# Another order of work for the last three tiles of an attention and sparse-network layer, and the flags' product first in every step

## The reference, cut to what matters

```python
x = x + attention(xn, Wq, Wk, Wv, Wo, rms_w) + ffn(xn, W_syn, b_syn, W_out, b_out, gamma, beta)

# attention: 16 heads of 32, linear attention in chunks of 128 with a decay for each head
inter = einsum('bhcd,bhde->bhce', qi * q_decay, kv)
scores = einsum('bhcd,bhsd->bhcs', qi, ki) * dmask
attn = rms_norm(inter + scores @ vi, rms_w) @ Wo

# ffn: ternary weights, of 2048 values of a row the 204 largest are kept
z = xn @ ternary(W_syn).T + b_syn
thresh = top_k(z, 204)[:, -1:]
hidden = where(z >= thresh, relu(z), 0)
out = layernorm(xn + hidden @ ternary(W_out).T + b_out) * gamma + beta
```

## Time and profile before

| | before |
|---|---|
| median of 3 runs | 943.66 us (943.35 to 943.76) |
| the profiled execution's own time | 945.01 us |
| its span, first to last instruction | 943.2 us |
| busy: TensorE, VectorE, ScalarE, GpSimd | 895.9, 748.7, 728.1, 659.6 us |

### The profile page before, as it was taken

The page is one execution under the profiler, slowest core; times in us unless marked ns, Lnnn a source line. Parts: engine busy times, 40 slices in busy tenths (PEclk is TensorE's granted clock), DMA queues, the critical chain, the costliest instruction groups (busy, mean ns, idle before and its releaser), DMA issues.

```text
span 943.2 us, 22295 instructions
## 1 busy us (share of the span) xinstructions
PE 895.9 (95%) x8307; PEld 437.6 (46%) x8307; DVE 748.7 (79%) x1955; ACT 728.1 (77%) x1321; POOL 659.6 (70%) x588
## 2 busy tenths in 40 slices
PE   4966899999999999999999999999999999999977
PEld 2532544444444444444444444444444444444434
DVE  5898877887777788778777878887787887878875
ACT  6799677987777788777777977777788777778663
POOL 1445578767677777776787777777767777877763
PEclk9989999999999999999999999999999999999999
DMA  9875653445344445534453544435344544444431
GB/s 336 242 190 102 113 102 69 89 91 100 81 84 96 95 63 91 102 83 85 92 101 72 88 91 91 89 81 102 71 87 91 101 80 80 101 87 73 80 77 36
DMA packets 255344, 93.98 MB, mean 100 GB/s; under 512 B 241408, under 2 KB 241664, under 8 KB 254464
## 3 DMA queue, kind: packets, MB, share of 16 engines
q1 hardware_dynamic: 251392, 85.11, 45.5%
q10 hardware_dynamic: 3840, 7.41, 2.2%
HBM read 24.34 MB, written 8.39 MB: 35 GB/s over the span
## 4 chain that ended last, share of the span: by engine, by line
PE 64%; ACT 12%; POOL 11%; issue 8%; DVE 3%; DMA 1%; ACTq 0%; DVEq 0%; POOLq 0%
PE proj L1123 35%; PE p_ffn L1237 8%; PE p_ffn L1267 7%; PE p_wo L1284 6%; ACT Pr L648 3%; PE rows L1193 3%; ACT hl L668 2%; PE rows L1183 2%; POOL area L859 1%; POOL hl L912 1%; DMA area<-in_L_attn_Wk_dram 1%; PE rows L1204 1%; POOL xhl L824 1%; POOL ahl L917 1%; POOL pair_b L936 1%
## 5 line engine op out<-in xcount | busy, mean ns | idle before, releaser
L1123 PE MATMUL proj<-wqkv,xT 128*128 128x512 f16 x1152 | 262.7, 384 | 2.7 <-ACT area L490 2.6
L1123 PE MATMUL proj<-wsynT,xT 128*128 128x512 f16 x1024 | 238.3, 381 | 3.6 <-ACT area L490 3.2
L912 POOL TENSOR_TENSOR hl<-area,hl 128x2048 f16<-128x2048 f32 x31 | 145.2, 4683 | 83.4 <-ACT hl L668 83.4
L1123 PEld LDWEIGHTS proj<-wqkv,xT 128*128 128x128 f16 x1152 | 110.2, 99 | 141.3 <-ACT area L490 14.8
L1123 PEld LDWEIGHTS proj<-wsynT,xT 128*128 128x128 f16 x1024 | 95.1, 98 | 119.6 <-issue 6.0
L1540 DVE SCALAR_TENSOR_TENSOR area<-proj,c,gb 128x512 f32<-128x512 f32 x128 | 95.3, 746 | 25.2 <-PE proj L1123 23.1
L1237 PE MATMUL p_ffn<-woutT,area 128*128 128x512 f16 x480 | 109.7, 379 | 0.0
L1267 PE MATMUL p_ffn<-woutT,area 128*128 128x512 f16 x480 | 108.5, 379 | 0.0
L620 ACT ACTIVATE diag<-ident,c 128x128 bf16<-128x128 f32 x32 | 12.8, 400 | 121.6 <-DVE c L1625 121.6
L1651 DVE MAX8 cand<-area 128x8 f32<-128x128 f32 x512 | 105.3, 277 | 1.1
L1284 PE MATMUL p_wo<-wo,ahl 128*128 128x512 f16 x384 | 88.6, 379 | 3.6 <-POOL ahl L917 2.2
(11 more groups left out here) (264 smaller groups left out, 1766.3 us busy)
## 6 DMA issues: line engine op xcount, KB each, us to landing
xrn<-in_L_attn_x_dram SPq DMA_DIRECT2D x32, 256.0 KB, 3.1
out_dram<-pair_b SPq DMA_DIRECT2D x29, 256.0 KB, 2.1
woutT<-in_L_ffn_W_syn_dram ACTq DMA_DIRECT2D x2, 1024.0 KB, 11.5
area<-in_L_ffn_W_syn_dram ACTq DMA_DIRECT2D x2, 1024.0 KB, 11.9
woutT<-in_L_ffn_W_out_dram SPq DMA_DIRECT2D x2, 1024.0 KB, 6.9
area<-in_L_attn_Wq_dram ACTq DMA_DIRECT2D x1, 1024.0 KB, 6.6
area<-in_L_attn_Wk_dram ACTq DMA_DIRECT2D x1, 1024.0 KB, 9.9
area<-in_L_attn_Wv_dram ACTq DMA_DIRECT2D x1, 1024.0 KB, 12.1
```

What stands on the lines that cost most here:

```text
L912: nc.gpsimd.tensor_tensor(hl[:, 1, :], src, hl[:, 0, :], ALU.subtract).then_inc(S["lo_ready"], 1)
L1123: last = nc.tensor.matmul(bank, xT[:, b.par, k, :], w, start=m == 0, stop=m == len(pairs) - 1)
```

## The change

It does three things. In every step the flags' product (`failures`) stands before the sixteen high-half products of the network instead of behind the tenth. In the last tiles the order of work on four engines is another: ScalarE copies T30's high half between the first and the second count; VectorE makes T30's low half in place of GpSimd; GpSimd joins T31's q ahead of tile 28's last two operations; TensorE takes T30's high-half products ahead of its attention products, T30's low-half products with the flags' product and the squares of T31 inside them, and T31's attention behind the first quarter of T31's network products. VectorE's small operations for T31's attention stand between the quarters of the hidden values instead of ahead of the flags. SyncE's program is the same.

```diff
--- before.py
+++ after.py
@@ -776,21 +776,21 @@
                 first_count(T31)
                 guess_moved(T31)
                 diagonal(T30)
+                hidden_high(T30, z[:, 0, :])
                 second_count(T31)
                 guess_settled(T31)
+                network_seeded(T30)
                 attention_high(T30)
                 projection_seeded(T30)
-                hidden_high(T30, z[:, 0, :])
                 third_count(T31)
                 out_stats(T29)
-                network_seeded(T30)
                 attention_out(T31)
                 out_shift(T29)
+                last_high(0)
                 diagonal(T31)
+                last_high(1)
                 projection_seeded(T31)
                 attention_high(T31)
-                last_high(0)
-                last_high(1)
                 out_normalised(T29)
                 out_stats(T30)
                 last_high(2)
@@ -1001,11 +1001,10 @@
 
             def last_steps():
                 wait(pool, "h_ready", T30, 1, 1)
+                q_joined(T31)
                 out_scaled(T28)
                 out_added(T28)
-                q_joined(T31)
                 attention_low(T30)
-                hidden_low(T30, z[:, 0, :])
                 out_root(T29)
                 squares_added(T31)
                 root_of_squares(T31)
@@ -1227,7 +1226,7 @@
                 wait(pe, "diag_ready", u, 1, 1)
                 nc.tensor.matmul(sbank[2][:, P:2 * P], ones16, diag, start=True, stop=True).then_inc(S["factors_spread"], 1)
 
-            def network_high(d, between=None, at=10):
+            def network_high(d, between=None, at=0):
 
                 wait(pe, "hiT", d, 16, 16)
                 wait(pe, "ffn_seeded", d, 1, 0)
@@ -1262,13 +1261,13 @@
 
                 wait(pe, "loT", d, 16, 16)
                 for k in range(NB):
-                    if k == 4 and between:
-                        between()
+                    if between and k in between:
+                        between[k]()
                     last = nc.tensor.matmul(p_ffn, hT[:, NB + k, :], woutT[:, k, :], start=False, stop=k == NB - 1,
                                             skip_group_check=True)
                 last.then_inc(S["ffn_done"], 1)
 
-            def attention_projected(u, between=None):
+            def attention_projected(u):
 
                 wait(pe, "ah_ready", u, 1, 1)
                 if u.n == 0:
@@ -1277,8 +1276,6 @@
                 wait(pe, "wo_seeded", u, 1, 0)
                 terms = [(l, w, g) for l, w in ((0, 0), (0, 1), (1, 0)) for g in range(HG)]
                 for m, (l, w, g) in enumerate(terms):
-                    if l and g == 0 and between:
-                        between()
                     if l and g == 0:
                         wait(pe, "al_ready", u, 1, 1)
                     last = nc.tensor.matmul(p_wo, ahl[:, l, g, :], wo[:, w, g, :], start=m == 0 and u.n == 0,
@@ -1327,12 +1324,13 @@
             def last_failures():
 
                 wait(pe, "fail_ready", T31, 1, 1)
-                wait(pe, "veR_ready", T31, 1, 1)
+                wait(pe, "sq_ready", T31, 1, 1)
                 nc.tensor.matmul(sbank[0][:, 1:2], ones16, failed, start=True, stop=True).then_inc(S["fail_all"], 1)
 
-            def last_sums():
-                wait(pe, "sq_ready", T31, 1, 1)
-                factors_spread(T31)
+            def last_squares():
+
+                wait(pe, "fail_count", T31, 1, 1)
+                squares_summed(T31)
 
             def last_flipped(q):
 
@@ -1348,6 +1346,7 @@
 
                 pe.wait_ge(S[name], q + 1)
                 wait(pe, "y_ready", T31, 1, 0)
+                wait(pe, "veR_ready", T31, 1, 1)
                 at = NB if name == "hq_low" else 0
                 for k in range(4 * q, 4 * q + 4):
                     for l in range(2):
@@ -1372,17 +1371,18 @@
                 network_low(T29)
                 factors_spread(T30)
                 scores(T31)
+                network_high(T30)
                 attention_projected(T30)
                 earlier_values(T31)
                 values(T31)
-                network_high(T30, lambda: squares_summed(T31), 11)
-                last_failures()
-                network_low(T30, last_sums)
-                attention_projected(T31, lambda: last_flipped(0))
-
+                network_low(T30, {10: last_failures, 14: last_squares})
+
+                last_flipped(0)
                 last_flipped(1)
                 last_network(0, "hq_high")
+                factors_spread(T31)
                 last_network(0, "hq_low")
+                attention_projected(T31)
                 last_network(1, "hq_high")
                 last_flipped(2)
                 last_network(1, "hq_low")
@@ -1851,6 +1851,12 @@
                 part = z[:, 1, q * 512:(q + 1) * 512]
                 nc.vector.scalar_tensor_tensor(part, part, thr, part, ALU.is_ge, ALU.mult).then_inc(S["hq_ready"], 1)
 
+            def hidden_low(u, src):
+
+                wait(dve, "hi_ready", u, 1, 1)
+                wait(dve, "loT", u, 16, 0)
+                nc.vector.tensor_tensor(hl[:, 1, :], src, hl[:, 0, :], ALU.subtract).then_inc(S["lo_ready"], 1)
+
             def last_low(q):
 
                 dve.wait_ge(S["hq_high"], q + 1)
@@ -1870,28 +1876,31 @@
                 row_factors(T30)
                 network_out(T29)
                 attention_normalised(T30)
+                hidden_low(T30, z[:, 0, :])
+                q_decayed(T31)
                 below(T31)
-                q_decayed(T31)
                 probs(T31, 0)
                 probs(T31, 1)
                 segments(T31, 0)
+                segments(T31, 1)
                 probs(T31, 2)
                 probs(T31, 3)
-                segments(T31, 1)
-                attention_added(T30)
                 segments(T31, 2)
                 segments(T31, 3)
-                selection(T31, lambda: mean_square(T31))
-                even_factor(T31)
-                row_factors(T31)
-                attention_normalised(T31)
+                selection(T31)
                 flags(T31, sbank[0][0:1, 1:2])
                 threshold(T31)
                 last_hidden(0)
                 network_out(T30)
+                mean_square(T31)
                 last_hidden(1)
+                even_factor(T31)
+                attention_added(T30)
                 last_low(0)
+                wait(dve, "att_added", T30, 1, 1)
+                row_factors(T31)
                 last_hidden(2)
+                attention_normalised(T31)
                 last_low(1)
                 last_hidden(3)
                 last_low(2)
```

## The result

| | before | after |
|---|---|---|
| median of 6 runs each, side by side | 943.5 us (942.59 to 944.92) | 947.11 us (946.84 to 948.73) |
| ratio, with its 95% interval | | 1.0041 (1.003 to 1.0052) |
| the profiled execution's own time | 945.01 us | 946.84 us |
| its span | 943.2 us | 945.0 us |

The changed kernel is 3.6 us slower by the medians, 3.9 us by the ratio, and the interval (2.8 to 4.9 us) lies beyond the 0.2% that a measurement of this kernel tells from none. So I compare the last tiles from a mark in the same place of both: S is the start of the last step's squares' product, F that of T31's flags' product, E the end of TensorE's last product.

A forecast was written before the change was run, and what follows sets the result against it. TensorE bounds the steps, and the end of its last product decides the difference. 0 in the steps, 0.7 us for F and 1.4 us behind it make 2.1 us more: 945.8 us, range 942.9 to 947.6 us.

The forecast's parts named there:

- Ordinary steps: Steps before the last tiles: moving the flags' product changes 0 us; bounds 2.0 us less to 0.9 us more.
- T30's chain: Last step, T30's search up to T31's flags: flags ready on VectorE at 921.2 in place of 922.29.
- SyncE's queue: Last tiles: high half's transpose, held behind tile 28's store, leaves at 907.4 instead of 910.94 and lands at 911.9.
- TensorE's gap: Behind T31's scores in the last tiles: TensorE idle for 4.1 us until T30's high half lands.
- The clock: Behind TensorE's new gap: clock falls, catching 2.8 us of high-half products, costing 1.4 us; bounds 0 and 3.4.
- F: Start of T31's flags' product in the last tiles: at 923.0, 0.7 us later than 922.34.
- S + 24.3 to 25.3: Sign in the last tiles: last flags' product at 922.5 to 923.5, VectorE ready 1 to 2 us before.
- Behind F: From flags' product to TensorE's end: waits for T31's attention make it F + 16.5, 1.4 us more than F + 15.04.
- Rival 1: Last tiles: clock doesn't fall or high half lands sooner; end 0.3 to 0.8 us later, 944.2 us; chance 0.20.
- Rival 2: Waits for T31's attention behind F: second clock fall, up to 1.7 us more, 947.5 us; chance 0.12.
- Rival 3: Behind F: TensorE never waits, T31's attention in time; 2.8 us earlier, 940.9 us; chance 0.13.
- Rival 4: Whole change doesn't act: the flags' gain is waited away elsewhere, 943.7 us; chance 0.08.

The follow-up runs named there:

- flags_steps: Kernel before with the flags' product first in the 28 ordinary steps only, T30's left behind the tenth product; 943.55 us, ratio 0.9998.
- tail_only: Changed kernel with the flags' product of the ordinary steps back behind the tenth product, T30's still first; 948.46 us, ratio 1.0055 to before.
- flags_all: Kernel before with the flags' product ahead of the high half's products in every step, T30's too; 942.7 us, ratio 0.9991.
- after_high_first: Changed kernel with SyncE's transpose of T30's high half ahead of tile 28's store; 945.73 us, ratio 1.0021 to before.
- after_filled: Changed kernel with 18 unread filler products while TensorE waits for T30's high half; 945.56 us, ratio 1.0023 to before.
- after_both_old_end: after_both with before's order of T31's attention on VectorE, ScalarE and TensorE; 944.71 us, ratio 1.0013 to before.
- after_both: Changed kernel with the high half's transpose ahead of tile 28's store and 9 unread filler products; 944.64 us, ratio 1.0009 to before.
- flags_all_filled: flags_all with 13 unread filler products in three TensorE waits behind T31's scores; 941.49 us, ratio 0.9983 to before.
- tail_new_filled: flags_all with reordered last tiles (early high half, transposes ahead of tile 28's store, low half first on GpSimd) and 9 filler products; 944.93 us, ratio 1.0018 to before.
- best: flags_all_filled with T31's flags' product and the spread moved three products into T30's low half; 940.83 us, ratio 0.9971 to before.

## Why the prediction was right, point by point

**The sign and the mechanism held; the loss was 3.6 us and not 2.1.** 947.1 us lies inside the range, near its upper end. In the last tiles' own measure it was 3.1 us.

- **Ordinary steps, 0: held as far as the medians tell.** `flags_steps` has the median of before (0.9998, within 0.1%). In the profiles the 29 steps between the second and the last squares' product take 790.9 us there and 792.5 in before, but before's profiled execution was itself 1.5 us above its median. All fourteen profiles point the same way: 792.5 and 793.1 us in the two kernels with the old place in the steps (before, `tail_only`), 790.7 to 792.0 in the twelve with the new one. A gain of about a us in the steps is not shown and not ruled out.
- **T30's chain: held.** With the flags' product first, T31's search starts 1.2 us sooner (`flags_all`: F 1.18 us sooner). In after, ScalarE's copy ended at S + 7.4 (forecast 7.5) and `below` started at S + 11.7 (11.5). The low half took 2.58 us on VectorE, where I took 2.3 from `below`; the other row, four narrow subtractions, gave 2.8. It began at 905.36, while GpSimd's addition (L943) ran until 905.78; in `flags_all` `below`, 2.34 us alone, took 2.59 from the same place beside GpSimd's joining. So the difference from 2.3 is probably this neighbour and not the operation. T31's flags were ready at S + 23.2 (23.0).
- **SyncE's queue: held.** Transpose at S + 9.4 (9.2), landing 4.5 us later. That the held store costs time was an argument only; `after_high_first` shows it, 1.9 us by the ratios.
- **TensorE's gap: held**, 4.37 us (4.1).
- **The clock: right in kind, the first mis-sized term.** It cost 1.9 us (5.34 less 3.46) and not 1.4, inside the bounds of 0 and 3.4. The fall was 6.8 us long, not 3.4, and caught the first 3.85 us of the high half's products (910.81 to 914.66) where I had put 2.8; half of 3.85 is the 1.9. Before has a fall too, 3.4 us that TensorE works through, about 1.7 us by the same halving, so of the difference between the two kernels the clock is only some 0.2 us. `tail_only` shows the term at 2.6 us by nothing but a later start of the same fall. The Trainium skill, "TensorE: Matmul & The Clock Gate", Part 1, has the rule that an idle stretch takes the clock down; the traces agree, and `after_filled`, where the gap is worked through at 1.00, shows that the gap is the cause.
- **F: forecast 0.7 us later, measured 1.5.** The difference is the clock (0.5), the landing (0.2) and the products between (0.1). That is S + 25.66, later than the S + 24.3 to 25.3 that I had named as a sign, and VectorE had been ready 2.4 us and not 1 to 2.
- **Behind F: forecast 1.4, measured 1.6, the second mis-sized term.** T31's attention products started at F + 7.8 (7.6) and TensorE's rest took 8.9 us, as forecast. What I had too short is GpSimd's root: it took 0.99 us here and not 0.55, so that the even factor came at F + 3.8 and not 3.4. It begins within VectorE's second quarter and ends 0.41 us behind it, in all six kernels with this order at the same 0.99 us; the other 32 roots of after's trace take 0.54 to 0.56. So the new order itself made this term longer. TensorE waited 0.42, 0.74, 0.27 and 1.44 us. All six kernels with this order show 16.66 or 16.67.
- **The rivals.** Rival 1, no fall: `after_filled` is what it describes, and it came to 945.6 us, more than its 944.2: from the marks its TensorE ends 1.2 us later than before's (F 0.4 us sooner, E - F 1.6 longer), where the rival had 0.3 to 0.8. Rival 2, a second fall, didn't come in after; `after_both_old_end` shows one of 3.4 us behind F, at 1.6 us of cost, close to the 1.7 named. Rival 3 needed T31's attention 3 us sooner; with the wait for the high half gone (`after_both`) E - F is still 16.67. Rival 4, no effect, is out by the interval.

Put together, in the last tiles against before: with the held transpose and the clock mended (`after_both`) F comes 0.9 us sooner, as far as VectorE's flags let it; those two cost 2.4 us of F - S together (1.89 and 2.33 alone, since VectorE is late next), and the order behind F 1.6: -0.9 + 2.4 + 1.6 is the 3.1 us measured. The 0.9 flatters the change, since before has its own fall of the clock. Against `flags_all_filled`, where the clock stays at 1.00 as in `after_both`, `after_both` is 3.0 us longer from S to E, 1.4 of it ahead of F, and 2.5 us longer by the ratios. The part that pays by itself is one line of the change (`flags_all`, 0.8 us); the rest takes it back and more. An order that keeps F early and T31's attention early at once was not found.

## What to carry to other kernels

Read a queue in order before moving work ahead: the high half was ready 2 us before it could leave, because a store that waited for another engine stood before it. Where the last tiles leave TensorE thin, what follows is done at half the clock, and a few products into a free bank can be cheaper than the fall (1.7 us in `after_filled`, 1.1 from `flags_all` to `flags_all_filled` in F - S), but not where another engine is late next (`tail_new_filled`); place the flag or sum that others wait for as early as its own input allows, and let TensorE work through the wait with what is already in memory. Price an order behind the last branch by the chain of small operations, each at its row's length, since there no engine's busy share tells anything, and look which operation of VectorE each of GpSimd's will meet.

## What the runs showed of the hardware that was not expected

VectorE and GpSimd held each other up in these traces when VectorE's operation had two inputs in SBUF. VectorE's decay of q (128x512) takes 0.74 us alone and 3.52 or 3.53 us when it begins within GpSimd's 128x2048 subtraction (4.07 us), ending some 0.5 us behind it both times; and it goes the other way round too: GpSimd's 128x512 addition took 3.20 us beside VectorE's `below` and 1.26 in after, where `below` itself took 3.35 for 2.34. GpSimd's root, 0.55 us, took 0.99 beside VectorE's second quarter. The Trainium skill, "SBUF — State Buffer", section Terms, describes this as an exclusive lock of the shared port pair, which blocks the loser fully; the traces agree, with these lengths. What decides is what the operation meets and not the engine alone: in `flags_all` and `best` T30's low half is on GpSimd too, 4.07 and 4.08 us, but later, beside operations of VectorE that keep their lengths.

The granted clock stayed at 0.50 for 3.4, 6.8 and 13.7 us; the last time it fell about 2 us into the wait of 12.69 us and rose about 3 us behind it. And it fell behind a stretch in which TensorE was not idle but thinly occupied, with 1.12 us of work in 3.42 in before. The same order of work can meet the fall 1.4 us sooner or later against its own products, which moved F by 0.7 us between `tail_only` and after.

Before's profiled execution lay 1.5 us above its median, and the profile of `flags_steps`, with the same last tiles (end of span at S + 45.04), has steps 1.6 us shorter at an equal median. So differences of a us between two profiles were read here only from a mark inside the last tiles.
